# Reordering three engines in the slice-attention stage: fx product ahead of the keys, VectorE's token work ahead of the exponentials' sums

## The reference, cut to what matters

```python
fx_mid = (x @ W_fx + b_fx)                      # per head [128 tokens, 64]
logits = ((x @ W_x + b_x) @ W_slice + b_slice) / temp
slice_weights = softmax(logits)                 # [128 tokens, 64 slices] per head
slice_token = einsum('nc,ng->gc', fx_mid, slice_weights)
slice_token = slice_token / (slice_weights.sum(over tokens) + 1e-05)
q, k, v = slice_token @ W_q, slice_token @ W_k, slice_token @ W_v
attn = softmax(q @ k.T * 64**-0.5)              # [64, 64] per head
out_x = slice_weights @ (attn @ v)
x = x + (out_x @ W_out + b_out)
```

## Time and profile before

| What | Value |
|---|---|
| median of 3 runs | 2773.0 us (2771.43 to 2773.26) |
| profiled execution, its own time | 2770.89 us |
| profiled execution, span of the trace | 2769.0 us |
| logits of the slice stage, first to last start | 776.5 to 1549.1 us, 128 graphs |
| busy in the stretch 950 to 1000 us | PE 49.89, DVE 43.62, ACT 32.36, POOL 25.83 us |

### The profile page before, as it was taken

How to read it: one execution, slowest core, us unless ns; L and a number is a source line. 1 busy time by engine, 2 the same in 40 slices (tenths; PEclk the granted TensorE clock), 3 DMA queues, 4 the chain that set the end, 5 groups by cost and what they waited for, 6 DMA issues and landing times. The chain is left out here.

```text
span 2769.0 us, 85746 instructions
## 1 busy us (share of the span) xinstructions
PE 2675.4 (97%) x28783; PEld 2143.5 (77%) x28784; DVE 1938.7 (70%) x6630; ACT 1461.0 (53%) x2930; POOL 1506.1 (54%) x2542
## 2 busy tenths in 40 slices
PE   8999999899979999999999899998998999999999
PEld 4666666599967888888878677777778999999888
DVE  6777777477778888888888577777864455544453
ACT  3555445455546666666666454444554444444444
POOL 5555555233335555555555447776752666666664
PEclk9999999999999999999999999999999999999999
DMA  1111111000000000000000011111422222222264
GB/s 53 35 34 34 34 31 47 2 0 0 0 2 0 0 0 0 0 0 0 0 0 0 21 41 58 58 54 54 129 72 67 78 77 76 77 78 81 70 202 143
DMA packets 158117, 118.26 MB, mean 43 GB/s; under 512 B 20150, under 2 KB 145593, under 8 KB 158010
## 3 DMA queue, kind: packets, MB, share of 16 engines
q1 hardware_dynamic: 140602, 81.02, 10.5%
q0 software_dynamic: 17408, 35.95, 3.8%
HBM read 68.36 MB, written 48.56 MB: 42 GB/s over the span
## 5 line engine op out<-in xcount | busy, mean ns | idle before, releaser
L2027 POOL DMA_INDIRECT token_y<-e_y,e_rows x288 | 295.2, 1025 | 78.8 <-issue 72.1
L2070 ACT ACTIVATE e_hidden<-e_ps,e_b1g 128x512 f32<-128x512 f32 x288 | 194.6, 688 | 258.3 <-PE e_ps L90 257.7
L1303 POOL DMA_INDIRECT sorted_z<-r_z,r_rows x256 | 263.8, 1031 | 67.2 <-issue 62.8
L842 POOL TENSOR_TENSOR s_sw<-s_expo,s_rsum 128x512 f32<-128x512 f32 x128 | 133.6, 1044 | 297.3 <-DVE s_rsum L1100 297.3
L2122 PE MATMUL e_ps<-expert_w,e_hidden 128*128 x2304 | 280.3, 275 | 0.0
L2122 PEld LDWEIGHTS e_ps<-expert_w,e_hidden 128*128 128x128 f32 x2304 | 273.9, 192 | 6.3
L514 DVE TENSOR_REDUCE a_V<-a_ps_s 128x8 f32<-128x1024 f32 x128 | 156.9, 1226 | 129.6 <-PE a_ps_s L394 129.6
L2199 DVE TENSOR_TENSOR e_biased<-e_ps,expert_b 128x512 f32<-128x512 f32 x72 | 49.8, 691 | 213.9 <-PE e_ps L2122 213.9
L394 PE MATMUL a_ps_s<-a_nT 16*128 16x128 f32 x2048 | 184.9, 298 | 0.1
L402 PE MATMUL a_ps_st<-a_topT,a_nT 17*128 17x128 f32 x2048 | 183.6, 297 | 0.1
L394 PEld LDWEIGHTS a_ps_s<-a_nT 16*128 16x128 f32 x2048 | 135.6, 187 | 45.5 <-issue 45.2
(11 more groups left out here) (400 smaller groups left out, 8094.8 us busy)
## 6 DMA issues: line engine op xcount, KB each, us to landing
e_z<-sorted_z SPq DMA_DIRECT2D x72, 260.0 KB
c_y<-token_y SPq DMA_DIRECT2D x22, 512.0 KB, 4.1
X<-in_x_dram SPq DMA_DIRECT2D x32, 256.0 KB, 2.8
a_adj<-in_adj_dram SPq DMA_DIRECT2D x32, 256.0 KB, 2.8
g_adj<-in_adj_dram SPq DMA_DIRECT2D x32, 256.0 KB, 2.9
out_dram<-X SPq DMA_DIRECT2D x32, 256.0 KB, 2.5
c_y_s<-token_y SPq DMA_DIRECT2D x10, 512.0 KB, 4.9
token_y<-e_y,e_rows POOLq DMA_INDIRECT x288
```

The lines of the kernel that those rows point to most:

```text
L842: nc.gpsimd.tensor_tensor(sw[p][:, :, :], expo[p][:, :, :], rsum[p][:, 1, :].unsqueeze(2).to_broadcast([T, HEADS, C]), ALU.mult).then_inc( ...
L1303: nc.gpsimd.indirect_dma_start(sh.sorted_z, bass.IndirectOffsetOnAxis(ap=rows[own][:, e * GB + piece:e * GB + piece + 1], axis=0), zr[own] ...
L2027: nc.gpsimd.indirect_dma_start(sh.token_y, bass.IndirectOffsetOnAxis(ap=rows[p][:, b:b + 1], axis=0), y[p][:, b, :], None).then_inc(y_scat ...
L2070: nc.scalar.activation(hidden[p][:, c, :], ps_1[c % 2][:, :], ACT.Gelu, bias=b1g[p][:, c:c + 1]).then_inc(s["hidden_done"], 1)
```

## The change

Nothing is computed in another way; instructions of `slice_phase` change their places in three queues. On TensorE the three `fx` products move from behind the turned shares to directly behind the logits; keys and turned shares follow them. On VectorE the slice tokens, the attention shares' sum and the low part of z go, in this order, ahead of the sum of the exponentials and its reciprocal. On GpSimd the scaling of `sw` moves behind the scaling of `share` and `rstd`. ScalarE's code is the same. Cut to its core:

```diff
@@ gpsimd step
-                if live(known, 2, n_graphs):
-                    pool.wait_ge(s["rsum_done"], t - 1)
...
-                    nc.gpsimd.tensor_tensor(sw[p][:, :, :], expo[p][:, :, :],
...
                 if live(known, 4, n_graphs):
                     pool.wait_ge(s["rsum2_done"], t - 3)
...
+                if live(known, 2, n_graphs):
+                    pool.wait_ge(s["rsum_done"], t - 1)
...
+                    nc.gpsimd.tensor_tensor(sw[p][:, :, :], expo[p][:, :, :],
@@ vector step
-                if live(known, 2, n_graphs):
-                    dve.wait_ge(s["expo_done"], t - 1)
...
-                    nc.vector.reduce_sum(rsum[p][:, 0, :], expo[p][:, :, :], AX.X).then_inc(s["sum_done"], 1)
-                    dve.wait_ge(s["sum_done"], t - 1)
-                    nc.vector.reciprocal(rsum[p][:, 1, :], rsum[p][:, 0, :]).then_inc(s["rsum_done"], 1)
                 if live(known, 3, n_graphs):
 
                     dve.wait_ge(s["u_done"], t - 2)
...
                     nc.vector.reduce_sum(rsum2[:, 0, :], att[:, :, :], AX.X).then_inc(s["sum2_done"], 1)
                     dve.wait_ge(s["sum2_done"], t - 3)
                     nc.vector.reciprocal(rsum2[:, 1, :], rsum2[:, 0, :]).then_inc(s["rsum2_done"], 1)
+                if live(known, 1, n_graphs):
+                    dve.wait_ge(s["zTh_done"], t)
+                    nc.vector.tensor_tensor(zTl[q][:, :], ps_z, zTh[q][:, :], ALU.subtract)\
+                      .then_inc(s["zT_done"], 1)
+                if live(known, 2, n_graphs):
+                    dve.wait_ge(s["expo_done"], t - 1)
...
+                    nc.vector.reduce_sum(rsum[p][:, 0, :], expo[p][:, :, :], AX.X).then_inc(s["sum_done"], 1)
```

More of the change, by code:

```diff
@@ L837, in step @@
                 p = k % 2
-                if live(known, 2, n_graphs):
-                    pool.wait_ge(s["rsum_done"], t - 1)
-                    if since(known, 4):
-                        pool.wait_ge(s["sw_turned"], t - 3)
-                    nc.gpsimd.tensor_tensor(sw[p][:, :, :], expo[p][:, :, :],
-                                            rsum[p][:, 1, :].unsqueeze(2).to_broadcast([T, HEADS, C]),
-                                            ALU.mult).then_inc(s["sw_done"], 1)
                 if live(known, 4, n_graphs):
@@ L860, in step @@
                                             ALU.pow).then_inc(s["rstd_done"], 1)
+                if live(known, 2, n_graphs):
+                    pool.wait_ge(s["rsum_done"], t - 1)
+                    if since(known, 4):
+                        pool.wait_ge(s["sw_turned"], t - 3)
+                    nc.gpsimd.tensor_tensor(sw[p][:, :, :], expo[p][:, :, :],
+                                            rsum[p][:, 1, :].unsqueeze(2).to_broadcast([T, HEADS, C]),
+                                            ALU.mult).then_inc(s["sw_done"], 1)
                 if live(known, 7, n_graphs):
@@ L883, in step @@
                                  True, True).then_inc(s["logits_done"], 1)
+                if live(known, 2, n_graphs):
+                    if since(known, 3):
+                        pe.wait_ge(s["fx_copied"], t - 2)
+                    split_matmul(nc, ps_f[:, :, :], (zTh[p][:, :], zTl[p][:, :]), [a[:, :] for a in wfx],
+                                 True, True).then_inc(s["fx_done"], 1)
                 if live(known, 4, n_graphs):
@@ L1093, in step @@
                                             ALU.subtract).then_inc(s["diff2_done"], 1)
-                if live(known, 2, n_graphs):
-                    dve.wait_ge(s["expo_done"], t - 1)
-                    if since(known, 4):
-                        dve.wait_ge(s["sw_done"], t - 3)
-                    nc.vector.reduce_sum(rsum[p][:, 0, :], expo[p][:, :, :], AX.X).then_inc(s["sum_done"], 1)
-                    dve.wait_ge(s["sum_done"], t - 1)
-                    nc.vector.reciprocal(rsum[p][:, 1, :], rsum[p][:, 0, :]).then_inc(s["rsum_done"], 1)
                 if live(known, 3, n_graphs):
@@ L1113, in step @@
                                             ALU.mult).then_inc(s["tok_done"], 1)
[L1114 to L1117, removed]
                 if live(known, 4, n_graphs):
@@ L1124, in step @@
                     nc.vector.reciprocal(rsum2[:, 1, :], rsum2[:, 0, :]).then_inc(s["rsum2_done"], 1)
+                if live(known, 1, n_graphs):
+                    dve.wait_ge(s["zTh_done"], t)
+                    nc.vector.tensor_tensor(zTl[q][:, :], ps_z, zTh[q][:, :], ALU.subtract)\
+                      .then_inc(s["zT_done"], 1)
+                if live(known, 2, n_graphs):
+                    dve.wait_ge(s["expo_done"], t - 1)
+                    if since(known, 4):
+                        dve.wait_ge(s["sw_done"], t - 3)
+                    nc.vector.reduce_sum(rsum[p][:, 0, :], expo[p][:, :, :], AX.X).then_inc(s["sum_done"], 1)
+                    dve.wait_ge(s["sum_done"], t - 1)
+                    nc.vector.reciprocal(rsum[p][:, 1, :], rsum[p][:, 0, :]).then_inc(s["rsum_done"], 1)
                 if live(known, 6, n_graphs):
```

## The result

The changed kernel takes 2822.58 us (median of 4 runs, 2820.47 to 2826.49) against 2773.13: a ratio of 1.0177, with a 95% interval of 1.0159 to 1.0194. It is slower by 49.5 us; 2832 was forecast, in a range of 2806 to 2852.

The account below looks back on a forecast made before the run. TensorE and VectorE, nearly in balance, were taken to bound the kernel. A round of 6.54 plus 0.02 for the branch, against 6.083, gives +0.477; times 124 that is 59 us, so 2832 us, range 2806 to 2852.

Parts of the forecast that it names:

- the cycle: Slice stage, one logits start to the next across TensorE, ScalarE and VectorE: 6.083 us a round would become 6.56.
- TensorE's part: Fx ahead of keys uncovers the fourth transpose's wait for `shareT`; scores start 0.24 to 0.29 us later.
- VectorE's part: Shares' sum and reciprocal ahead of `zTl` lengthen the stretch from `rnorm` to the logits from 1.03 to 1.59 us.
- the two bounds: At the fourth transpose on TensorE, an uncovered weight load adds 0.06 or 0.11 us before the scores.
- the logits' 28 waits for `zTl`: TensorE's logits before the change, waiting for VectorE: 7.3 us over 28 rounds, read as the engines nearly in balance.
- GpSimd, X and `sw`: Later `sw` on GpSimd and X's addition, ending near 1.0 of the next round, delay nothing: no cost.
- two round lengths: Next logits start at 6.49 or 6.54 us, from `rnorm` at 4.90 or 4.95 plus 1.59.
- One (the wait covered): Fourth transpose's wait for `shareT` is covered; scores at 2.66, logits at 6.07, no change, 2772 us; chance 0.07.
- two (TensorE's gain survives): TensorE's products alone set the round; its 0.18 us gain gives 5.90 a round, 2751 us; chance 0.05.
- Four (the wait half covered): VectorE's chain alone, wait at L914 half covered: scores near 2.9, round 6.3, +27, 2800 us; chance 0.06.
- Three, the clock: Short TensorE pauses lower its clock in a tenth of the rounds: +42 us on top, 2874; chance 0.05.

Follow-up runs that it names:

- the version that eased both: Against the kernel before: three transposes behind the logits, the fourth behind fx; exponentials' sum last, `zTl` ahead of shares' sum, GpSimd's new order; 2762.61 us, ratio 0.9962.

## Why the prediction was right

**Sign and mechanism.** Both parts of the cycle are shown: undoing TensorE's part takes back the whole loss, undoing the place of the shares' sum takes back 27 us of it, and one more copy on ScalarE lengthens the round by 0.266 us.

**TensorE's part.** The keys were to start at 1.49 and did; the load of the fourth transpose was to start at 2.82, it is 2.83; scores at 3.08 to 3.13, they are at 3.09. The wait for `tokT` is gone as said. One detail was off without consequence: the third transpose was to be ready at 2.54 and loads at 2.62, 0.12 behind the end of `key` rather than 0.05. It carries two waits. From the fourth load to the scores it was 0.26, the lower of the two bounds (0.20 + 0.06).

**VectorE's part.** `rnorm` was to start at 4.90 to 4.95 and starts at 4.89; the stretch from there to the logits was to be 1.59 and is 1.60. The round was to be 6.49 or 6.54 and is 6.49 in this place.

**Two readings of before.** The prediction took the logits' 28 waits for `zTl` as waits for VectorE. The next round shows one of them:

```profile
1008.06 0.19 PEld L88 LDWEIGHTS s_ps_l<-s_wlogit_high,s_zTh 128*128 128x128 f32 x1 [0.26 <-DVE s_zTl L1116]
```

`zTl` had ended at 1007.75, 0.31 earlier, and this is the first round of a loop pass; 28 in 115 rounds is one for each pass. So these waits belong to the pass, not to VectorE. Where VectorE does hold TensorE in before is a line that the prediction did not use, the transposed tokens' wait for `tok` in every round:

```profile
PEld s_ps_t L973 <- DVE s_tok L1111: 20.4, 115, 1.3
```

Both leave the sum as it is, for it was taken from the timeline; the second supports its reading of two engines nearly in balance. In after this wait is gone but for one round.

**GpSimd, X and `sw`.** Costed at nothing. GpSimd's change alone gives nothing; X's addition stood in no run by itself, but it ends at 1.07 of the round of after, and no line of the waits view is a wait for it.

**The size.** 59 us were forecast, 49.5 measured, 50.9 in the stage. The term that was too large is the one from the round to the sum: I took the upper of two round lengths, 6.54, added 0.02 and multiplied by 124, +0.477 each. The steady distance grew by 6.524 - 6.088 = 0.436; 124 of those are 54. The rest lies where the pipeline fills: the first four distances between logits were 4.93, 4.99, 7.39 and 7.32 and are 4.80, 4.28, 5.85 and 6.08, together 3.6 us shorter, where the prediction had charged nothing for three of them and the full +0.477 for the fourth. The other 123 grew by 54.5, and 54.5 - 3.6 = 50.9.

**The parts do not add up, and I did not say so.** TensorE's move costs 39 us with VectorE as before; with VectorE's new order it costs 49.5. The shares' sum ahead of `zTl` costs 38 us by itself, nothing where the exponentials' sum goes last and TensorE is as before, and 27 us in the changed kernel. That fits a cycle in which the longest way counts and the earlier bounds absorb part of each new one.

**The rivals.** One (the wait covered) and two (TensorE's gain survives) did not occur; the waits above contradict them. Four (the wait half covered) had scores near 2.9 and a round of 6.3; they are at 3.09 and 6.52. Three, the clock, is excluded: the steady window of after shows a granted clock of 1.00, the 2.4 GHz level (as the stretch from 1000 to 1500 us does), with TensorE busy in 47.95 us where it was 49.89:

```profile
950.00:1000.00 50.00, 47.95 (x669) 38.80 (x666) 41.02 (x140) 30.02 (x78) 24.43 (x54) 1.00 0.00 0
```

## What to carry to other kernels

In a software pipeline written out by hand, read a round as a cycle of "finished, picked up, copied, picked up" across engines, and keep enough independent work between a product and the instruction that waits for its copied result; here keys, two copies and two pick-ups needed 1.33 us and the change left 0.98. Moving work that fills a visible wait can take away the cover of a longer wait that no view showed because it was covered. And when two engines are in balance, easing one of them alone gives nothing, as the run with only the exponentials' sum moved shows; the version that eased both got a little faster (ratio 0.9962). Its order on TensorE alone, with VectorE as before, was not run.

## What was not expected of the hardware

The start of a loop pass costs time, and how much differs from kernel to kernel. In the kernel before, TensorE and VectorE each idle about 0.25 us there (the load at L88 above; VectorE's first instruction of a round, L1047, 28 times in 115 rounds). In the run with TensorE's order alone the round that ends there is 6.55 long against 6.29, and the next one 6.47; in the changed kernel, where the logits wait for VectorE anyway, starts at 1004.33, 1010.82, 1017.31, 1023.83 and 1030.43 are 6.49, 6.49, 6.52 and 6.60 apart. That the loop's branches are the cause is inferred from the period of four rounds; no run changed the loop.

A transpose with one wait loads 0.05 us behind the end of the copy it waits for, the one with two waits 0.12 us, and the one with three waits, in the version with three transposes first, 0.12 us. That the number of waits makes the difference was not tried by itself.
